# A linear-attention block with float16 instead of float32r projections: scales found before the weights are split

## The reference, cut to what matters

```
x = L0_attn_x                                   # (8, 1024, 512) float32
qkv = layernorm(x) @ qkv_w.T + qkv_b            # 16 heads of 32
q, k = relu(q) + 1e-6, relu(k) + 1e-6
kv, k_cum = cumsum(k outer v), cumsum(k)        # causal, over 1024 positions
out = (q . kv) / max(q . k_cum, 1e-6)
x = x + out @ out_w.T + out_b
h = layernorm(x); s = max(abs(h)) / 127         # one scale for the whole array
x = x + (round(h / s) @ w_int8.T) * s * w_scale + ffn_bias
```

## Time and profile before

| what | value |
|---|---|
| median of 3 runs | 1302.74 us (1299.88 to 1304.51) |
| the profiled execution | 1300.72 us |
| its span, first to last instruction | 1298.9 us |
| mean granted TensorE clock | 0.978 of full |
| TensorE matmuls busy | 1199.1 us (92%), 10927 instructions |
| VectorE busy | 1086.8 us (84%) |
| POOL busy | 701.7 us (54%) |
| ScalarE busy | 568.6 us (44%) |
| phase two | about the last 100 us of the span |

### The profile page before, as it was taken

One profiled execution on the slowest core, in us unless ns is written; L12 is line 12 of the kernel. 1 busy time (PEld: TensorE's weight loads), 2 busy tenths in 40 slices (PEclk: granted clock), 3 DMA queues, 4 the chain that ended last, 5 costly groups with the idle time before them and its releaser, 6 DMA issues. The chain is left out here.

```text
span 1298.9 us, 31782 instructions
## 1 busy us (share of the span) xinstructions
PE 1199.1 (92%) x10927; PEld 1058.7 (82%) x10927; DVE 1086.8 (84%) x2425; ACT 568.6 (44%) x1130; POOL 701.7 (54%) x847
## 2 busy tenths in 40 slices
PE   5789999999899999999899999999999999974998
PEld 3689888888888888898888888888898888953665
DVE  6578889888898888888888889888888898767887
ACT  4434444444344444444444444443344444422553
POOL 3355555555555555555455555555555555540887
PEclk9799999999999999999999999999999999986999
DMA  5123223222222232232222222223222231140994
GB/s 210 50 58 82 82 66 87 73 74 79 67 79 73 74 82 75 81 82 73 77 74 74 74 74 76 74 74 84 74 83 77 73 84 41 48 155 17 317 349 177
DMA packets 73950, 120.92 MB, mean 93 GB/s; under 512 B 16449, under 2 KB 16961, under 8 KB 73794
## 3 DMA queue, kind: packets, MB, share of 16 engines
q1 hardware_dynamic: 72544, 117.51, 30.6%
q10 hardware_dynamic: 1250, 1.32, 0.4%
HBM read 36.97 MB, written 31.46 MB: 53 GB/s over the span
## 5 line engine op out<-in xcount | busy, mean ns | idle before, releaser
L380 POOL TENSOR_SCALAR_AFFINE_SELECT am_hi<-am_hi 128x512 f16<-128x512 f16 x256 | 174.0, 680 | 385.4 <-DVE am_lo L826 385.4
L430 PE MATMUL unit<-xt_hi,w_hi 128*128 128x256 f32 x1024 | 306.2, 299 | 8.9 <-DVE xt_lo L801 8.0
L430 PE MATMUL unit<-xt_hi,w_lo 128*128 128x256 f32 x1024 | 292.1, 285 | 5.2 <-issue 5.2
L430 PE MATMUL unit<-xt_lo,w_hi 128*128 128x256 f32 x1024 | 291.9, 285 | 0.0
L430 PEld LDWEIGHTS unit<-xt_hi,w_hi 128*128 128x128 f32 x1024 | 197.1, 192 | 23.4 <-DVE xt_lo L801 12.9
L358 POOL TENSOR_SCALAR q_t<-q_t,eps_scaled 128x256 f32<-128x256 f32 x128 | 123.2, 962 | 147.9 <-ACT q_t L633 147.9
L430 PEld LDWEIGHTS unit<-xt_lo,w_hi 128*128 128x128 f32 x1024 | 197.3, 193 | 2.5
L430 PEld LDWEIGHTS unit<-xt_hi,w_lo 128*128 128x128 f32 x1024 | 196.9, 192 | 0.0
L633 ACT ACTIVATE q_t<-unit,qk_bias_scaled,qk_scale 128x256 f32<-128x256 f32 x128 | 72.2, 564 | 232.7 <-PE unit L430 232.7
L380 POOL TENSOR_SCALAR_AFFINE_SELECT am_lo<-am_lo 128x512 f16<-128x512 f16 x256 | 173.6, 678 | 0.0
L826 DVE SCALAR_TENSOR_TENSOR am_lo<-sc,am_hi 128x512 f16<-128x512 f32 x256 | 163.5, 679 | 9.3 <-ACT am_hi L661 9.1
(11 more groups left out here) (141 smaller groups left out, 2932.6 us busy)
## 6 DMA issues: line engine op xcount, KB each, us to landing
stack<-qk_hi SPq DMA_DIRECT2D x512, 64.0 KB, 2.0
xs<-x SPq DMA_DIRECT2D x64, 256.0 KB, 2.7
stack<-qk_lo SPq DMA_DIRECT2D x256, 64.0 KB, 2.0
out<-res SPq DMA_DIRECT2D x64, 256.0 KB, 3.3
x_spill<-xs SPq DMA_DIRECT2D x56, 256.0 KB, 2.1
w_lo<-x_spill SPq DMA_DIRECT2D x44, 256.0 KB, 4.0
w_hi<-x_spill SPq DMA_DIRECT2D x12, 256.0 KB, 4.4
stack<-qkv_wt SPq DMA_DIRECT2D x2, 768.0 KB, 7.8
```

The costliest lines, as they stand in the source:

```text
L380: ins = pool.affine_select(out=am[:, r, :, :], in_=am[:, r, :, :], compare_op=ALU.is_ge, fill=0.0, base=0, pattern=[[0, HG], [1, CHUNK]], ...
L430: mm = pe.matmul(dst[:, 0:GT], wp[:, k, f:f + P], xp[:, g % 2, k, :], start=(n == 0), stop=(n == len(terms) - 1))
```

## The change

All projection operands become float16 halves in place of float32r ones: `w_hi`, `w_lo`, `wo_hi`, `wo_lo`, `xt_hi`, `xt_lo`, `at_hi`, `at_lo`.
- So that float16 holds them, the input is multiplied by 16 (inside the layer norm's constants), the qkv weights by a power of two per third, `out_w` by a power of its own. The matmul's result then has the scale that the features need: the scale operand of `features` and of `finish_values` and one of `den_max`'s two go. The residual gets one instead.
- The weights can only be split when the scales are there: all squares first, then five small steps, then three wide splits by column blocks (k, q, v), 2048 elements a row each; the first query/key units wait for their own third alone.
- `out_w` is loaded at the start, in one DMA, behind the qkv weights and ahead of input chunks 2 to 7; squares, sums, a root and six small steps (`out_of`) give its scale.
- Phase two's ring is a buffer of its own.

The core of the diff:

```diff
-    FEATURE_STEPS = 7
-    POWER_STEPS = 13
+    WEIGHT_STEPS = 5
+    FEATURE_STEPS = 8
+    POWER_STEPS = 14
+    OUT_STEPS = 6
+    X_TOP = 2.0 ** 4
+    W_TOP = 2.0 ** 10
-        w_hi = buf(top, "w_hi", [P, EC, 3 * E], F32R)
+        w_hi = buf(top, "w_hi", [P, EC, 3 * E], F16)
-        x1 = [w[:, k, j * E:(j + 1) * E].bitcast(F32) for w in (w_lo, w_hi) for k in range(EC) for j in range(3)][:RING]
+        x1_ring = buf(top, "x1_ring", [P, RING, E])
...
 SP
                 for i in range(EC):
+                    sp.dma_start(stage[:, i, :], qkv_wt[i * P:(i + 1) * P, :]).then_inc(w_loaded[i], 16)
+                sp.dma_start(wo_stage, out_wt.rearrange("(c p) n -> p c n", p=P)).then_inc(wo_loaded, 16)
...
+                sp.wait_ge(w_lo_done, 3)
                 stack_parts(0, 0, 0)
                 stack_parts(0, 0, 1)
-                sp.wait_ge(w_lo_done, EC + 2)
+                sp.wait_ge(wo_lo_done, 1)
...
 TensorE
-                pe.wait_ge(w_lo_done, EC)
+                pe.wait_ge(wo_squared, 1)
+                for k in range(EC):
+                    mm = pe.matmul(misc[:, :], ones_bf[:, :], wo_squares[:, k, :], start=(k == 0), stop=(k == EC - 1))
+                mm.then_inc(wo_sums_ready, 1)
                 for i in range(QK):
+                    if i % HG == 0:
+                        pe.wait_ge(w_lo_done, 1 + i // HG)
                     project(0, 0, ("qk", i))
...
 ScalarE
                     act.activation((k_t if i < HG else q_t)[:, g % 2, i % HG, :], unit[:, unit_bank[("qk", i)], 0:GT], ACT.Relu,
-                                   bias=qk_bias_scaled[:, f:f + 1],
-                                   scale=(qk_scale[:, 1:2] if i < HG else qk_scale[:, 0:1])).then_inc(qk_done, 1)
+                                   bias=qk_bias_scaled[:, f:f + 1]).then_inc(qk_done, 1)
...
+                for i in range(EC - 1):
                     act.wait_ge(w_loaded[i], 16)
+                    if i >= 2:
+                        act.wait_ge(sums_ready, i)
+                    act.activation(squares[:, i % 2, :], stage[:, i, :], ACT.Square).then_inc(squares_ready[0], 1)
+                act.wait_ge(wo_loaded, 16)
+                act.activation(wo_squares, wo_stage, ACT.Square).then_inc(wo_squared, 1)
                 act.wait_ge(sums_read, 3)
                 act.activation(bounds[:, 0:3], sums[:, 0:3], ACT.Sqrt, scale=2.0 * E * 1.01).then_inc(bounds_ready, 1)
+                act.wait_ge(power_step, WEIGHT_STEPS)
+                for n in (1, 0, 2):
+                    act.activation(w_hi[:, :, n * E:(n + 1) * E], stage[:, :, n * E:(n + 1) * E], ACT.Copy,
+                                   scale=w_scale[:, n:n + 1]).then_inc(w_hi_done, 1)
+                act.wait_ge(wo_sums_read, 1)
+                act.activation(wo_bound[:, :], sums[:, 3:4], ACT.Sqrt, scale=1.01).then_inc(wo_bound_ready, 1)
                 act.wait_ge(power_step, FEATURE_STEPS)
                 for i in range(2):
                     features(0, 0, i)
...
 VectorE
-                    dve.scalar_tensor_tensor(out=v1[:, g % 2, i, :, 0:D],
-                                             in0=unit[:, unit_bank[("v", i)], :].rearrange("p (h d) -> p h d", h=HEADS),
-                                             scalar=v_scale[:, 0:1], in1=v_bias_scaled[:, :].rearrange("p (h d) -> p h d", h=HEADS),
-                                             op0=ALU.mult, op1=ALU.add).then_inc(v_done, 1)
+                    dve.tensor_tensor(v1[:, g % 2, i, :, 0:D],
+                                      unit[:, unit_bank[("v", i)], :].rearrange("p (h d) -> p h d", h=HEADS),
+                                      v_bias_scaled[:, :].rearrange("p (h d) -> p h d", h=HEADS), ALU.add).then_inc(v_done, 1)
-                    dve.tensor_tensor(xs[:, c % CB, :], misc[:, :], xs[:, c % CB, :], ALU.add).then_inc(x1_ready, 1)
+                    dve.scalar_tensor_tensor(out=xs[:, c % CB, :], in0=misc[:, :], scalar=out_unscale[:, 0:1], in1=xs[:, c % CB, :],
+                                             op0=ALU.mult, op1=ALU.add).then_inc(x1_ready, 1)
-                                      den_eps[:, 0:1], v_scale[:, 0:1], ALU.max, ALU.mult).then_inc(den_ready, 1)
+                                      den_eps[:, 0:1], None, ALU.max).then_inc(den_ready, 1)
...
+                step(dve.tensor_scalar(w_scale[:, :], inverse[:, :], W_TOP, None, ALU.mult))
...
                 assert n[0] == FEATURE_STEPS
+                for i, k in enumerate((1, 0, 2)):
+                    dve.wait_ge(w_hi_done, i + 1)
+                    dve.scalar_tensor_tensor(out=w_lo[:, :, k * E:(k + 1) * E], in0=stage[:, :, k * E:(k + 1) * E],
+                                             scalar=w_scale[:, k:k + 1], in1=w_hi[:, :, k * E:(k + 1) * E],
+                                             op0=ALU.mult, op1=ALU.subtract).then_inc(w_lo_done, 1)
...
                 assert n[0] == POWER_STEPS
+                dve.wait_ge(wo_sums_ready, 1)
+                dve.tensor_reduce(sums[:, 3:4], misc[:, :], AX.X, ALU.max).then_inc(wo_sums_read, 1)
+                dve.wait_ge(wo_bound_ready, 1)
...
                 ln_moments(0, 1, True)
```

More of the change, by code:

```diff
@@ L173, in build @@
         with ExitStack() as one:
-            wo_hi = buf(one, "wo_hi", [P, EC, E], F32R)
-            wo_lo = buf(one, "wo_lo", [P, EC, E], F32R)
+            wo_hi = buf(one, "wo_hi", [P, EC, E], F16)
+            wo_lo = buf(one, "wo_lo", [P, EC, E], F16)
             qk_bias = buf(one, "qk_bias", [P, QK])
@@ L189, in build @@
             rstd = buf(one, "rstd", [P, GROUP])
-            xt_hi = buf(one, "xt_hi", [P, 2, EC, GT], F32R)
-            xt_lo = buf(one, "xt_lo", [P, 2, EC, GT], F32R)
+            xt_hi = buf(one, "xt_hi", [P, 2, EC, GT], F16)
+            xt_lo = buf(one, "xt_lo", [P, 2, EC, GT], F16)
             q_t = buf(one, "q_t", [P, 2, HG, GT])
@@ L204, in build @@
             stack = buf(one, "stack", [P, 2, 2, HEADS, GT], F16)
[L207 to L213 removed]
+            slab = stack[:, :, :, :, :].rearrange("p b a h t -> p (b a h t)")
+            stage = slab.bitcast(F32)[:, 0:3 * EC * E].rearrange("p (c n) -> p c n", c=EC)
+            wo_stage = slab.bitcast(F32)[:, 3 * EC * E:4 * EC * E].rearrange("p (c n) -> p c n", c=EC)
+            squares = q_t[:, :, :, :].rearrange("p a g t -> p (a g t)").bitcast(BF16)[:, 0:6 * E].rearrange("p (a n) -> p a n", a=2)
+            bias_row = k_t[:, :, :, :].rearrange("p a g t -> p (a g t)")[0:1, 0:3 * E]
+            bias_squares = am_hi[:, :, :, :].rearrange("p a g t -> p (a g t)").bitcast(BF16)[0:1, 0:3 * E]
+            wo_squares = am_lo[:, :, :, :].rearrange("p a g t -> p (a g t)").bitcast(BF16).rearrange("p (c n) -> p c n", c=EC)
+            ffn_i8 = slab.bitcast(I32)[:, 0:E].rearrange("p (c n) -> p c n", c=EC)
             ones_bf = buf(one, "ones_bf", [P, P], BF16)
@@ L231, in build @@
             attn = buf(one, "attn", [P, HEADS, D])
-            at_hi = buf(one, "at_hi", [P, EC, P], F32R)
-            at_lo = buf(one, "at_lo", [P, EC, P], F32R)
+            at_hi = buf(one, "at_hi", [P, EC, P], F16)
+            at_lo = buf(one, "at_lo", [P, EC, P], F16)
             stats2 = buf(one, "stats2", [P, 6])
@@ L696, in _ @@
                     split_x(0, c)
-                for h in range(2):
-                    act.wait_ge(w_loaded[h], 32)
-                    act.activation(wo_hi[:, 2 * h:2 * h + 2, :], stage[h][:, 0:2 * E].rearrange("p (c n) -> p c n", c=2),
-                                   ACT.Copy).then_inc(w_hi_done, 1)
+                act.wait_ge(out_step, OUT_STEPS)
+                act.activation(wo_hi[:, :, :], wo_stage, ACT.Copy, scale=wo_scale[:, 0:1]).then_inc(wo_hi_done, 1)
                 for j in range(GROUP):
@@ L894, in _ @@
                     split_x(0, c)
-                for i in range(EC):
-                    if i == EC - 1:
-                        dve.wait_ge(w_loaded[i], 16)
-                        dve.wait_ge(sums_ready, i)
-                        dve.tensor_tensor(squares[:, i % 2, :], stage[i], stage[i], ALU.mult).then_inc(squares_ready[1], 1)
-                    dve.wait_ge(w_hi_done, i + 1)
-                    dve.tensor_tensor(w_lo[:, i, :], stage[i], w_hi[:, i, :].bitcast(F32), ALU.subtract
-                                      ).then_inc(w_lo_done, 1)
+                dve.wait_ge(w_loaded[EC - 1], 16)
+                dve.wait_ge(sums_ready, EC - 1)
+                dve.tensor_tensor(squares[:, (EC - 1) % 2, :], stage[:, EC - 1, :], stage[:, EC - 1, :], ALU.mult
+                                  ).then_inc(squares_ready[1], 1)
                 dve.wait_ge(sums_ready, EC + 1)
@@ L943, in _ @@
                     finish_values(0, 0, j)
-                for h in range(2):
-                    dve.wait_ge(w_hi_done, EC + h + 1)
-                    dve.tensor_tensor(wo_lo[:, 2 * h:2 * h + 2, :], stage[h][:, 0:2 * E].rearrange("p (c n) -> p c n", c=2),
```

(4 more changed lines are left out.)

69 lines of the change are left out of this document (40 added, 29 removed).

## The result

| what | before | after |
|---|---|---|
| median | 1302.69 us (4 runs) | 1286.72 us (4 runs, 1286.03 to 1287.84) |
| the profiled execution | 1300.7 | 1287.0 |
| its span | 1298.9 | 1285.2 |
| mean granted TensorE clock | 0.978 | 0.967 |

The ratio is 0.988, interval 0.9861 to 0.9899: 16 us faster. The prediction said 1265, a gain of 38. The measured value lies inside its range (1244 to 1288), just short of the upper end, but less than half of the forecast gain came, and the account of it does not hold.

The account below looks back on a forecast made before the run. TensorE's stretch (14.4 us) and that of VectorE and POOL (20.7) were taken to pace each 35.2 us pair in turn. Pairs save 42 us, the start costs 5.5: 1300.7 - 42 + 5.5 = 1264, stated as 1265, range 1244 to 1288.

Parts of the forecast that it names:

- The steps: TensorE's matmul steps with float16 operands: 0.108 us for 256 columns, 0.215 for 512, no longer first step.
- Features near 34 us: At the start: ScalarE's first features come at 34.2 us instead of 27.21, queued behind the root of wo's bound.
- The start's transposes: At the start: TensorE's transposes at 38.65 us move to 43.4, or 45.2 if the clock drops meanwhile.
- `t1` still ends with `v_lo`: In the odd chunk: VectorE's two-element t1 stays held until POOL's v_lo subtractions end.
- VectorE's stretch: The 20.7 us of a pair paced by VectorE and POOL: dropped pointer scalars save 0.15 us on the path.
- the fourth saves TensorE's work throughout ... I take 2.1: Fourth pair of a batch, taken as paced by TensorE throughout: saves 2.1 us, seven times, 14.7 us.
- rival *Slower: Rival, chance 0.05: more TensorE idle time lowers the granted clock; about 1310 us at a tenth of the stage at half clock.
- rival *Less: Rival, chance 0.17: 256-column float16 steps stay at 0.118 us, or qk_lo/mask interleaving costs more; 1284 us.
- "Left: 1.0": TensorE's stretch of a normal pair: 1.2 us saved, less 0.2 lost at the masks, leaves 1.0.
- The gate of the masks: TensorE's outputs wait for POOL's last mask, 0.65 us of room; qk_lo between masks costs 0 to 0.3, taken 0.2.
- three first steps 0.3: TensorE's stretch: the slower first step of a unit, surplus about 0.11 us, disappears three times, saving 0.3 us.
- "+4 to +7, taken +5.5": Start of the kernel: splits wait for the weight scales, delaying features and transposes; net cost 4 to 7 us, taken 5.5.

Follow-up runs that it names:

- mask_before: Kernel before with its loop, leaving out the am_lo causal mask in the fourth round of each even chunk: 1297.1 us (0.9984).
- mask_after: Changed kernel with its loop, leaving out the am_lo causal mask in the fourth round of each even chunk: 1274.2 us (0.979).

## Why the prediction was wrong

**Right.** The steps: 0.109 for a forecast 0.108, 0.215 for 0.215; a float16 weight load of 100 ns under them (L446). Features near 34 us: 33.36. The start's transposes, forecast at 43.4 to 45.2: 44.26. `t1` still ends with `v_lo`. VectorE's stretch is 20.53 us (671.38 to 691.91) for 20.74, 0.2 where 0.15 was forecast. TensorE's idle share from 200 to 1000 us rose to 7.5%, forecast towards 8%.

**The step that failed first: "the fourth saves TensorE's work throughout ... I take 2.1", for seven pairs, 14.7 us.** The prediction read VectorE's 1.81 us before `xt_lo` in the earlier trace rows as a wait for TensorE's work through `xt_hi`. With the loop written out that idle time is gone in the kernel before, where `xt_lo` now follows without a gap:
```profile
614.20 0.65 DVE L846 TENSOR_REDUCE recent_stats<-xs 128x1 f32<-128x512 f32 x1
614.77 0.68 DVE L799 TENSOR_TENSOR xt_lo<-unit,xt_hi 128x512 fp32r<-128x512 f32 x1
```
So it was the jump's (in the kernel after it is 1.63 us, by VectorE's own issue), and TensorE has two such stops. A jump's 3.5 us go with it, and a fourth pair then saves what the others do: (137.8 - 134.6) / 4 = 0.8. There are five jumps, not seven. And what the pair could have saved TensorE gave up in the clock: five falls against two. Jumped batches give 1.3 us where 5.5 was forecast; their three normal pairs account for 2.3, so the fourth is 1 us slower than before: 0.8 saved, 1.4 more lost to the clock a jump (2.0 against 0.6 on average), 0.4 more at the jump itself (3.4 against 3.0).

The rival *Slower* had the right resource and the wrong place. It asked whether 4% more idle time spread over the stage would lower the clock, took 0.99 over 800 us as evidence, and gave 0.05. The clock did not fall from spread idle time: written out, TensorE is busy 752 of 800 us and the clock stays at 1.00. It fell at the jumps, in the kernel after 0.3 to 1.4 us behind the end of a stop of 2.3 to 2.7 us. The Trainium skill, TensorE: Matmul & The Clock Gate, The HAM clock gate, has the throttled state as the default that activity releases; the traces agree between 200 and 1000 us, with 1.00 in the written-out kernel and the falls of the looped ones only behind stops. Open is why the kernel before fell at two of its jumps only. Its stops are somewhat shorter (2.5 to 3.6 us together at a jump, 3.4 to 4.3 after), but those of the two jumps with a fall (2.5 and 3.1) are not its longest, and in mask_before the falls come at two other jumps.

The rival *Less* gave 1284, close to the 1286.7 measured, but not by its first condition, since the narrow steps did fall to 0.109. Its second one, a dearer interleaving of `qk_lo` and the masks, did come true and is a part of the error (below). That the total comes out so near is luck: most of the missing gain is at the jumps, which this rival did not have.

**The second: "Left: 1.0" of TensorE's stretch, in every normal pair.** Measured 14.39 to 13.83, 0.56. The gate of the masks was taken at 0.2 from a range of 0 to 0.3; it is 0.37 at the outputs (664.07, where 663.70 would follow the transposes as usual) and 0.07 more in their first step behind the stop (0.19 us for 0.12). That is 0.44, and mask_after puts 0.45 a pair on it. The mechanism was the one forecast, `qk_lo` between the masks, and one mask went from 0.63 to 0.82. TensorE's own saving is 0.94 for 1.2: 0.57 up to the outputs without the gate (6.72 us behind the release in the earlier trace rows, 663.70 - 657.55 = 6.15 now) and 0.37 from there to the last `keys_values` (7.02 and 6.65). Of the 0.26 that are missing, 0.07 is that first step. Another 0.13 is in the term "three first steps 0.3", which was too large. Before, the unit behind the first `keys_values` started 0.03 us behind its last matmul, so the slow first step only gave back what had been gained there. Now that distance is 0.11 (667.57 to 668.10 is 0.53 for four matmuls where it was 0.45), and the one between the last score matmul and the output projection 0.08 instead of 0.03. The last 0.06 are small differences in the steps. Pairs: -0.77 for -1.15; 23 of them, 9 us.

**The sum**: 38.5 us forecast for seven batches and 12.3 measured is the error; the start (2.9 for 5.5) and the last batch with phase two (4.3 for about 4) lie within a few us. The start's own terms, +4.8 to +6.6 less 1.3, give 3.5 to 5.3 and not the "+4 to +7, taken +5.5" of the text. Measured, the transposes moved by 5.6 (38.65 to 44.26) and 2.7 of it came back by the first key transposes.

**What lay under it.** The prediction saw `t1` held until `v_lo` ended and used it only to say where nothing could be gained. The experiments show its size: 20 us in either kernel. With it TensorE's saving turns into a longer wait for `state` (0.8 to 1.5 us); with it and POOL's order out of the way the same change is worth 27 us instead of 22. So of the 22 us that are missing, the jumps with their clock account for 6 (22 against 16) and VectorE's chain for 5 (27 against 22); the masks' gate takes 12, of which 0.2 a pair, 5 us, was in the forecast. These were measured on different bases and need not add up.

## What to carry to other kernels

Where two engines pace a pair in turns, a saving on one is first the other's wait: before summing savings, list for every later operation the engine that it will then wait for, and price the smallest room first (here 0.65 us at the masks). Do not read the idle time around a loop's jump as a wait for work: here it went when the loop was written out. Count in what the clock does behind it. A tiny operation that takes a microsecond is the best row in a profile: ask what holds it, and whether it can be written with fewer SBUF tensors or by single columns.

## What the runs showed of the hardware

- VectorE operations of two elements that read two SBUF tensors took 1.04 and 1.11 us beside POOL's `v_lo`, ending within 20 ns of its ends; as one-element column operations with pointer scalars some 0.23 us each (0.45 for two). A two-element operation with one input took 0.56 us in the same place, ending 0.03 us behind POOL's first instruction, and the 512-wide normalising 0.99 instead of 0.55, so one-input operations are held as well.
- POOL is slowed in turn: a mask takes 0.64 us alone and 0.82 beside VectorE's `qk_lo`.
- TensorE's clock fell to half at all five jumps of the kernel after (stops of 2.3 to 2.7 and 1.0 to 1.6 us) and at two of five in the kernel before (the second and the fifth; in mask_before at the first and the fourth); in the written-out kernel after it did not fall between 80 and 1100 us.
- A jump of the loop cost 3.5 us on average in the kernel before and 5.4 in the one after. Of that 3.0 and 3.4 are left without the steps at half clock.
